# Routed feed-forward after attention on one core: the second layer's weights are split in the attention part and multiplied in three reduced-precision products

## What is computed

```python
x = x + xattn(layernorm(x), ctx)     # 16 heads of 32; keys = values = context; @ W_out.T + b
x = x + attn(layernorm(x), ...)      # 32x32 self attention, low-rank projections, rotary part, @ Wo + b
xf = layernorm(x)                    # the routed layer:
idx = argmax(softmax(xf @ Wg + bg))  # one expert of 8 for each row
h = gelu(xf @ W1[idx] + b1[idx], exact)
x = x + h @ W2[idx] + b2[idx]        # W1, W2: 8 x 512 x 512
```

## Time and profile before

| | |
|---|---|
| runs | 808.64 us median (805.21, 808.64, 811.38) |
| profiled execution | 810.45 us, its span (first to last instruction) 808.6 us |
| mean granted clock of PE | 0.970 of full speed |
| busy share of the span | PE 90%, PE weight loads 69%, DVE 72%, ACT 54%, POOL 42% |
| transfers | 129.06 MB, mean 160 GB/s; SP's queue 51.2% of the engines' time |
| chain that ended last | PE 62%, DVE 14%, DMA 8%, issue 6%, ACT 5% |

### The profile page before, as it was taken

How to read it: one execution, slowest core, us unless ns; L and a number is a source line. 1 busy time by engine, 2 the same in 40 slices (tenths; PEclk the granted TensorE clock), 3 DMA queues, 4 the chain that set the end, 5 groups by cost and what they waited for, 6 DMA issues and landing times.

```text
span 808.6 us, 26299 instructions
## 1 busy us (share of the span) xinstructions
PE 731.3 (90%) x10502; PEld 554.5 (69%) x10502; DVE 582.9 (72%) x1184; ACT 435.3 (54%) x1085; POOL 337.4 (42%) x687
## 2 busy tenths in 40 slices
PE   4978899998999989999999898999897879999997
PEld 3635677777877867777778687787686546666664
DVE  3458376878878788778787777877547547788983
ACT  2335265756667557565666565765423435555552
POOL 1202343435344434353444434443404357866652
PEclk9899699999999999999999999999998989999999
DMA  9954266567576765775756647561241997544420
GB/s 278 343 119 106 67 149 143 137 159 183 133 175 145 161 152 141 159 180 126 188 140 158 156 123 180 140 162 56 82 167 53 329 389 284 180 152 137 142 104 4
DMA packets 114376, 129.06 MB, mean 160 GB/s; under 512 B 14478, under 2 KB 81294, under 8 KB 114256
## 3 DMA queue, kind: packets, MB, share of 16 engines
q1 hardware_dynamic: 105984, 109.26, 51.2%
q0 software_dynamic: 5520, 16.26, 5.7%
q10 hardware_dynamic: 2752, 1.86, 0.9%
HBM read 114.77 MB, written 14.42 MB: 160 GB/s over the span
## 4 chain that ended last, share of the span: by engine, by line
PE 62%; DVE 14%; DMA 8%; issue 6%; ACT 5%; SPq 2%; POOL 2%; ACTq 1%; DVEq 0%; POOLq 0%
PE stage_banks L1642 9%; PE stage_banks L539 6%; DMA keys<-in_ctx 6%; PE stage_banks L541 5%; PE stage_banks L540 5%; PE scores L590 5%; PE att_bank L614 4%; PE stage_banks L533 3%; PE scores L600 3%; PE scores L1620 2%; PE scores L1622 2%; PE scores L1621 2%; SPq L457 2%; DVE k_t L1080 2%; PE stage_banks L546 2%
## 5 line engine op out<-in xcount | busy, mean ns | idle before, releaser
L875 ACT ACTIVATE prob<-scores,negmax 128x257 f32<-128x257 f32 x256 | 118.5, 476 | 45.5 <-DVE negmax L1090 45.5
L539 PE MATMUL stage_banks<-qkv_hi,operand_hi 128*128 128x398 f32 x256 | 98.1, 383 | 4.3 <-DVE operand_lo L1094 4.2
L1080 DVE STREAM_TRANSPOSE k_t<-keys 128x512 f32<-128x512 f32 x128 | 86.4, 686 | 16.9 <-DMA keys<-in_ctx 16.9
L540 PE MATMUL stage_banks<-qkv_lo,operand_hi 128*128 128x398 f32 x256 | 88.6, 346 | 0.0
L1090 DVE TENSOR_REDUCE negmax<-scores 128x2 f32<-128x514 f32 x128 | 82.9, 678 | 7.7 <-PE scores L590 7.4
L541 PE MATMUL stage_banks<-qkv_hi,operand_lo 128*128 128x398 f32 x256 | 88.4, 345 | 0.0
L600 PE MATMUL scores<-consts,prob 128*128 128x128 f32 x512 | 77.1, 278 | 12.1 <-ACT prob L875 12.1
L1642 PE MATMUL stage_banks<-w_all,hidden 128*128 x184 | 82.8, 592 | 0.6 <-ACT hidden L1695 0.6
L614 PEld LDWEIGHTS att_bank<-prob_t,context 128*32 128x32 f32 x4096 | 45.9, 114 | 50.0 <-issue 36.3
L600 PEld LDWEIGHTS scores<-consts,prob 128*128 128x128 f32 x512 | 60.1, 142 | 26.1 <-ACT prob L875 22.6
L1738 DVE TENSOR_TENSOR w_lo<-w_all,w_hi 128x512 fp32r<-128x512 f32 x89 | 76.8, 921 | 0.8 <-ACT w_hi L1674 0.3
(11 more groups left out here) (260 smaller groups left out, 1664.0 us busy)
## 6 DMA issues: line engine op xcount, KB each, us to landing
keys<-in_ctx SPq DMA_DIRECT2D x256, 128.0 KB, 4.6
context<-in_ctx SPq DMA_DIRECT2D x64, 512.0 KB, 4.6
w_all<-in_L_ffn_W SPq DMA_DIRECT2D x16, 1024.0 KB, 10.1
b<-in_L_ffn_b SPq DMA_DIRECT2D x23, 256.0 KB
norm_scratch<-norm SPq DMA_DIRECT2D x16, 256.0 KB
x_tile<-in_x SPq DMA_DIRECT2D x8, 256.0 KB, 3.0
x_pair<-in_x SPq DMA_DIRECT2D x8, 256.0 KB
x_scratch<-x_tile SPq DMA_DIRECT2D x8, 256.0 KB, 2.3
```

Source lines behind the costliest of these rows:

```text
L539: pe.matmul(to, op_hi[op][:, c, :], w_hi[name][:, c, columns], start=(c == 0), stop=False)
L540: pe.matmul(to, op_hi[op][:, c, :], w_lo[name][:, c, columns], start=False, stop=False)
L875: act.activation(prob[pair][:, gg, :], scores[:, g, 0:J], ACT.Exp, bias=negmax[b % 2][:, g:g + 1], accum_out=sums[t % 2][:, g, bl:bl + 1]) ...
L1080: dve.transpose(dst, src).then_inc(keys_turned, 1)
```

## The change

- **Second layer in three products.** `w_all` holds, for each expert, the high and the low part of W2 instead of W1 and W2. ACT cuts gelu's result into a high part (`hidden_hi`), DVE forms `hidden_lo`, each in two halves, and `second_layer` makes 12 F32R products in place of 4 plain ones.
- **W2 is split ahead of time.** In the attention part, at every 17th step from step 112 on, one of 32 pieces (128 rows of an expert's W2, 256 KB) is loaded by ACT's queue, copied to its high part and subtracted to its low part by POOL, and 512 KB stored to a DRAM scratch by ACT's queue. Expert 0 is loaded back at step `STEPS * (B + 1)`, experts 1 to 5 as buffers of the attention part come free, 6 and 7 in the expert part.
- **W1 is loaded for each slot**, 1 MB, into two buffers `first_raw`, two slots ahead.
- **The second bias** is fetched by index in the attention part (`TAKE_B2`, POOL) and added to x2 by POOL before x2 is stored (`ADD_B2`); `add_bias` and `load_bias` go. The stores of x2 and norm3 move from SP's queue to ACT's (`STORE2`, `STORE3`). x has five buffers (`NX = 5`), and `load_x` no longer waits for norm3.
- `move_first` goes from DVE to ACT, the order on ACT and DVE in a slot is another, there are more fill products (`RANK` 2 to 8, `SLOTS` 6 to 10), and buffers lie elsewhere.

```diff
-EARLY = 2
+LOAD_OF = (0, 1, 1, 2, 2, 2, 3, 4)
+NX = 5
+TAKE_B2, ADD_B2, STORE2, STORE3 = 109, 114, 117, 106
+SPLIT_FIRST, SPLIT_EVERY = 112, 17
+SPLIT_HI, SPLIT_LO, SPLIT_STORE = 10, 12, 15
-BEFORE = {..., "RANK": 2, "SLOTS": 6, "FIRST": 9}
+BEFORE = {..., "RANK": 8, "SLOTS": 10, "FIRST": 9}
 # SP
         def load_x(t):
-            if t >= 4:
-                until.wait_ge(x2_stored[t % 4], 16 * (t // 4))
-                until.wait_ge(normed_r, t - 3)
+            if t >= NX:
+                until.wait_ge(x2_stored[t % NX], 16 * (t // NX))
...
-                sp.dma_start(x2_dram[t * P:(t + 1) * P, :], x_tile[t % 4][:, :])...
-                sp.dma_start(norm3_dram[t * P:(t + 1) * P, :], norm3[:, :])...
             if step == STEPS * (B + 1):
...
-                for e in range(EARLY):
+                until.wait_ge(w2_stored, 16 * G)
+                load_expert(sp, 0)
+                sp.dma_start(first_raw[0][:, :, :], ins["L0_ffn_W1"][0]...).then_inc(first_loaded[0], 16)
+                until.wait_ge(xout_done, T)
+                until.wait_ge(att_used, T)
+                until.wait_ge(w2_stored, 16 * E * G)
+                for e in (1, 2):
+                    load_expert(sp, e)
+                until.wait_ge(qkv_done, 4 * T)
+                until.wait_ge(self_scored, T)
+                for e in (3, 4, 5):
                     load_expert(sp, e)
 # ACT, attention part
+            t = tile_at(step, STORE3, LATER["STORE3"])   # wait normed_r t+1, store norm3
+            t = tile_at(step, STORE2, LATER["STORE2"])   # wait x2_biased t+1, store x2
+            n = split_at(step, 0)
+                until.wait_ge(w2_made, 2 * n)
+                act.dma_start(w2_whole, ins["L0_ffn_W2"][e, m * P:(m + 1) * P, :]).then_inc(w2_loaded, 16)
+            n = split_at(step, SPLIT_STORE)
+                until.wait_ge(w2_made, 2 * n + 2)
+                act.dma_start(w2_dram[e, :, :, m, :], w2_part).then_inc(w2_stored, 16)
 # POOL, attention part
+            t = tile_at(step, TAKE_B2, LATER["TAKE_B2"])
+                until.wait_ge(expert_known, t + 1)
+                pool.indirect_dma_start(b2_rows[:, :], None, ins["L0_ffn_b2"][:, :], ...top_at...).then_inc(b2_taken, 16)
+            t = tile_at(step, ADD_B2, LATER["ADD_B2"])
+                until.wait_ge(b2_taken, 16 * (t + 1))
+                pool.tensor_tensor(x_tile[t % NX][:, :], x_tile[t % NX][:, :], b2_rows[:, :], ALU.add).then_inc(x2_biased, 1)
+            n = split_at(step, SPLIT_HI)
+                until.wait_ge(w2_loaded, 16 * (n + 1))
+                pool.tensor_copy(w2_part[:, 0, :].bitcast(F32R), w2_whole).then_inc(w2_made, 1)
+            n = split_at(step, SPLIT_LO)
+                pool.tensor_tensor(w2_part[:, 1, :].bitcast(F32R), w2_whole, w2_part[:, 0, :], ALU.subtract).then_inc(w2_made, 1)
 # SP, expert part
+        def load_first(s):
+            if s >= 2:
+                until.wait_ge(w1_low, G * (s - 1) - 2)
+                until.wait_ge(w1_low_first, 2)
+            at = sp.value_load(of_slot_i[0:1, s:s + 1], ...)
+            sp.dma_start(first_raw[s % 2]..., ins["L0_ffn_W1"][bass.ds(at, 1), :, :]...).then_inc(first_loaded[s % 2], 16)
+        load_first(1)
         for s in range(SLOTS):
+            if s == 0:   # wait for norm3 rows of 4 slots and x2 rows of 4 slots
+            if s in (0, 2):
+                load_expert(sp, 6 + s // 2)
             if s + 2 < SLOTS:
-                load_bias(s + 2)
+                load_first(s + 2)
 # PE, second_layer
             for m in range(G):
-                done = pe.matmul(bank[:, :], hidden[s % 2][:, m, :], w_of[..., 1, m, :]..., start=(m == 0), stop=(m == G - 1))
+                until.wait_ge(hidden_high, 2 * s + m // 2 + 1)
+                pe.matmul(bank[:, :], hi[:, m, :], high, start=(m == 0), stop=False)
+                pe.matmul(bank[:, :], hi[:, m, :], low, start=False, stop=False)
+                until.wait_ge(hidden_low, 2 * s + m // 2 + 1)
+                done = pe.matmul(bank[:, :], lo[:, m, :], high, start=False, stop=(m == G - 1))
 # ACT, expert part
         for s in range(SLOTS):
             if s + 1 < SLOTS:
-                split_rows(s + 1)
-                split_first(s + 1)
+                split_first(s + 1, range(3))
+            move_first(s)
+            if s + 1 < SLOTS:
+                split_first(s + 1, (3,))
+            for half in range(2):   # two gelus, wait for them, one cut of 128x256 into hidden_hi
+            if s + 2 < SLOTS:
+                split_rows(s + 2)
 # DVE, expert part
         for s in range(SLOTS):
             if s + 1 < SLOTS:
                 lower_first(s + 1, range(G))
             if s:
                 add_rows(s - 1)
             if s + 1 < SLOTS:
                 move_b1(s + 1)
+            lower_hidden(s)         # two subtractions of 128x256
+            if s + 2 < SLOTS:
+                lower_rows(s + 2)
 # POOL, expert part: add_bias gone; before the gathers it waits for all x2 rows, as before
```

More of the change, by code:

```diff
@@ L189, in part_at, with split_at, program @@
     return -1, 0
+def split_at(step, offset):
+    n, rest = divmod(step - offset - SPLIT_FIRST, SPLIT_EVERY)
+    return n if rest == 0 and 0 <= n < E * G else -1
 def units_at(step):
     return [n for n, at in enumerate(UNIT_AT) if at == step]
-def program(nc, ins, out, const_at, x2_dram, norm3_dram):
+def program(nc, ins, out, const_at, x2_dram, norm3_dram, w2_dram):
     ctx = ExitStack()
@@ L346, in program @@
     const_loaded, tables_loaded, last_loaded = signal("const_loaded"), signal("tables_loaded"), signal("last_loaded")
-    x_loaded = [signal(f"x_loaded{i}") for i in range(4)]
+    x_loaded = [signal(f"x_loaded{i}") for i in range(NX)]
     context_loaded = [signal(f"context_loaded{i}") for i in range(4)]
@@ L1505, in program @@
     first = [sb(f"first{i}", [P, FI]) for i in range(2)]
-    hidden = [sb(f"hidden{i}", [P, G, P]) for i in range(2)]
+    first_raw.append(sb("first_raw1", [P, G, FI]))
     routing = ExitStack()
@@ L1517, in program @@
     routing.close()
-    b2_loaded = [signal(f"b2_loaded{i}") for i in range(2)]
+    hidden_hi, hidden_lo = ([sb(f"{n}{i}", [P, G, P], F32R) for i in range(2)] for n in ("hidden_hi", "hidden_lo"))
+    hidden = [sb(f"hidden{i}", [P, G, P]) for i in range(2)]
     rows_gathered = [signal(f"rows_gathered{i}") for i in range(NR)]
@@ L1541, in attention_over, with rows_stored, loaded_to, first_layer_loaded @@
         until.wait_ge(rstd_r, T)
-    def loaded_to(until, s, layers):
+    def rows_stored(until):
+        for i in range(NX):
+            until.wait_ge(x2_stored[i], 16 * ((T - 1 - i) // NX + 1))
+    def loaded_to(until, s):
         for e in range(min(s, E - 1) + 1):
-            until.wait_ge(expert_loaded[e], 16 if e == EARLY else 32)
-        if layers == 2 and s >= EARLY:
-            until.wait_ge(second_loaded, 16)
+            until.wait_ge(expert_loaded[LOAD_OF[e]], 16 * LOAD_OF.count(LOAD_OF[e]))
+    def first_layer_loaded(until, s):
+        until.wait_ge(first_loaded[s % 2], 16 * (s // 2 + 1))
     def expert_sync_program():
@@ L1636, in second_layer @@
                 until.wait_ge(known, PUT_AT)
-            loaded_to(until, s, 2)
+            loaded_to(until, s)
             until.wait_ge(known, EXPERTS)
             place = pe.value_load(at_i[0:1, s:s + 1], min_val=0, max_val=E - 1)
+            hi, lo = hidden_hi[s % 2], hidden_lo[s % 2]
             for m in range(G):
-                until.wait_ge(gelu_done, G * s + m + 1)
-                done = pe.matmul(bank[:, :], hidden[s % 2][:, m, :], w_of[:, bass.ds(place, 1), 1, m, :].rearrange("p a n -> p (a n)"),
-                                 start=(m == 0), stop=(m == G - 1))
+                high, low = (w_of[:, bass.ds(place, 1), part, m, :].rearrange("p a n -> p (a n)").bitcast(F32R) for part in range(2))
+                until.wait_ge(hidden_high, 2 * s + m // 2 + 1)
[3 more added lines that the diff above has]
+                done = pe.matmul(bank[:, :], lo[:, m, :], high, start=False, stop=(m == G - 1))
             done.then_inc(second_done, 1)
```

231 lines of the change are left out of this document (121 added, 110 removed).

## The result

The changed kernel took **853.34 us** (median of four: 846.53, 848.43, 858.25, 862.44) against 810.01 for the kernel before on the same chip: ratio **1.052, 95% interval 1.0463 to 1.0576**. Forecast were 797 us and a range of 783 to 811. The execution of 862.44 us ran in a slower state (granted clock 0.938, where the two fastest have 0.953), and the ratio leaves it out. It is the one that was profiled (span 860.3): the other three are 4 to 16 us shorter, about 0.3 to 1.2 us a tile.

A forecast was written before the change was run, and what follows sets the result against it. PE was taken to bound the expert slots, with full DMA in the first slots and small waits in attention. From 810.45 us, -15.2 - 3 + 2 + 0.7 - 6 + 5 + 3 = -13.5 gave 797 us, range 783 to 811.

The forecast's parts named there:

- The failed step: Attention part, POOL: added subtractions, copies, gathers and additions, 114 us of work, cost +3 us, bounds 0 and +15.
- The sign of being wrong: Attention part: a tile of 33.5 us or more, with ACT or POOL in the chain, would show the forecast wrong.
- Second layer, -15.2: Expert part: 12 reduced products replace four plain ones, 0.66 us saved in each of 23 slots, -15.2 us.
- slot stays near 7: Rival, expert part: late W1 or ACT's round keeps slots at 6.7 to 7.0 us, total 804 to 811; chance 0.22.
- ACT's thin slack: Expert part: ACT's move ends at 11.1 us, next turn_first due at 11.9; slack 0.8 us, holding barely.
- three passes for four: Second layer: counting passes through the array, reduced products would save 19.8 us instead of the 15.2 taken.
- First slots, -3: Start of expert part: of 9.3 us lost, some 6 come back as W1 loads late; -3, bounds -9 and +3.
- End of attention and routing, +2, bounds 0 and 4: The last tile's bias chain (fetch, landing, addition, store) delays ACT's W1 cuts and the first gather: +2 us.
- SP unblocked, -6, bounds 0 and -9: Attention part: without SP's wait for norm3, keys come in time and PE's 7.7 us at L784 can go: -6.
- ACT's 96 issues, +5: Attention part: 64 W2 issues and 32 stores, 42 us on ACT, an eighth reaching PE: +5, bounds 0 and +35.
- The rival with a chance of 0.13: ACT's issues: at 1.0 us each, a third reaching PE, 96 cost 32 us, total 824; chance 0.13.
- POOL's added work, +3: Attention part: 114 us more on POOL, busy 13.8 of 33, with long gaps: +3, bounds 0 and +15.

The follow-up runs named there:

- neither: The changed kernel without the second bias's fetch and addition and without the split of W2 (loaded directly): 787.7 us, ratio 0.9732 to the kernel before.
- Run 11: The changed kernel with split, bias addition and x2 store later, plus SP loading W1 of slots 1 and 2 first, experts 6 and 7 in pieces: 802.4 us.
- kernel 1: The changed kernel without the indexed fetch and addition of the second bias, x2 stored without it: 809.7 us, ratio 1.0018 to the kernel before.
- run 12: Run 11's kernel with the last but one tile's x2 store later and experts 3 to 5 loaded one by one, 4 and 5 after bias fetches: 803.9 us.
- Run 13: The kernel before with x2 and norm3 stored from ACT's queue and five x buffers, nothing else of the change: 794.5 us, ratio 0.9823.
- run 7: "neither" plus the split's 64 transfers from ACT's queue, loads waiting for nothing, no split work on POOL: 792.3 us, ratio 0.9805 to the kernel before.
- run 6: "neither" plus the split's transfers from ACT's queue, each load waiting for the store two steps before it, nothing on POOL: 867.55 us, ratio 1.0732.

## Why the prediction was wrong

**The failed step** is, in its words, on POOL: "its order carries last-key copies, the reciprocal deviation and the wait for b2_taken: +3, bounds 0 and +15". I named the wait, named what stands behind it, and then priced the pair as if little more than POOL's busy time counted. POOL's second wait, that of `SPLIT_HI` for its piece, has no term at all. The sign of being wrong that I had named, a tile of 33.5 us or more with ACT or POOL in the chain, is what came: 36.7, and POOL is 17% of the chain of after. What the runs put in its place, from 787.7 ("neither") up to 853.3:

| fetch | split | us | tile, us | PE's wait for `norm_x`, us |
|---|---|---|---|---|
| none | none | 787.7 | 31.5 | none |
| none | POOL's work alone | 795.4 | 32.1 | 2.3 |
| none | transfers alone | 792.3 | 31.9 | none |
| as changed | none | 794.6 | 31.8 | 3.5 |
| none | as changed | 809.7 | 33.5 | 7.0 |
| late | late | 807.1 | 33.05 | 6.5 |
| late | as changed | 821.7 | 33.9 | 9.9 |
| as changed | late | 837.6 | 34.95 | 20.5 |
| as changed | as changed | 853.3 | 36.7 | 26.8 |

The last row's tile and wait are those of the execution of 862.44 us.

Time over 787.7 and PE's wait for `norm_x` grow together, 2.0 to 3.4 us of time for one of wait. Part of that factor is the lower clock behind a wait; PE's waits for key copies (7.5 us in after, none in "neither") and for `norm_w` (7.4 and 5.2) and the end of the attention part have their share, which I have not divided up. That is a correlation over nine kernels; the separate causes are the differences between rows.

**Why fetch and split cost 65.6 together and 6.9 and 22.0 alone.** The runs show that it is so and that the place of the addition and of the x2 store behind it decides most of it: moved, they win back 31.6 of the fetch's 43.6 us. The traces give a reason, which is an argument from them. ACT waits for `shift_x` in every tile of "neither" too (24.1 us, 14 times, longest 1.9), and PE never waits for it: there is slack. Without the split the fetch lands 4.1 us after its issue (median, 100 to 540 us) and POOL waits at most 2.5 us for it; ACT's wait grows to 35.8 us and PE's only to 3.5. With the split the landing takes 5.9 us, POOL's wait reaches 5.9, and a cast and a subtraction stand between it and the deviation: the slack is used up and what comes on top reaches PE. How much is due to the later landing and how much to the added operations is not separated; no run had the fetch beside the transfers alone. Nor is how much came by ACT's store of x2, which waits for the addition ahead of the norm: in the tile shown it was issued at 210.59 us, and the norm behind it began only at 215.33, after the deviation.

**The other terms.**
- *Second layer, -15.2*: right. 6.43 us a slot was forecast as 6.4 (23 x 0.62 = 14.3 measured), so no other engine is in the way: the rival "slot stays near 7" is out, ACT's thin slack held, and the DMA share of 0.83 is the forecast 82%. The products start 0.234 us apart (759.38 to 761.95 for 11 steps); the alternative of three passes for four, -19.8, was wrong, as the earlier trace rows said.
- *First slots, -3*: 38.5 us against 37.5, of which four slots at 6.43 against 7.05 explain -2.5. So the surplus over four slots rose from 9.3 to 12.8 us: +3.5, just outside my upper bound of +3. W1 of slot 2 was late, as said: ACT waited 8.5 us for it in after, and PE 4.9 us for the move that stands behind those cuts in ACT's order, where I had said about 5. What failed is that the rest of the stall did not go: PE also waited 2.7 us for ACT's move in slot 0, and its granted clock was 0.67 from 700 to 720 us. Run 11 confirms the part of W1.
- *End of attention and routing, +2, bounds 0 and 4*: wrong, and by the same error. The chain I had written down (fetch, landing, addition, store) was priced with a landing of "3 or so". Experts 1 and 2, and then 3 to 5, 10 MB, are on the queues there, and the trace of after has
```profile
645.14 1.27 POOL L1446 TENSOR_TENSOR x_pair<-x_pair,staged_c 128x512 f32<-128x512 f32 x1 [8.04 <-DMA staged_c<-in_L_ffn_b,top_at]
675.53 0.81 ACT L859 ACTIVATE norm<-x_tile,shift_r,rstd_r 128x512 f32<-128x512 f32 x1 [12.16 <-DMA norm_scratch<-norm]
```
  8.04 us for one bias and 12.16 for the store of norm3, 256 KB each. The second is also in kernel 1, without any bias (11.4 us). In after it has a twin: ACT's store of x2, next ahead in its order, was issued at 675.10 us, when POOL had made the addition that it waits for (673.81 + 1.26), so a prompt landing of norm3 alone would have gained next to nothing there. From the last ranking product to slot 0 pass 17.2 us in place of 13.1, and more lies ahead of that product. I don't put one number on it, since run 12 shows that the wait moves when it is chased.
- *SP unblocked, -6, bounds 0 and -9*: right in kind, too small, and outside my bound. Run 13 has 14.5 us for it alone (809.06 to 794.51; 10 to 18 by the interval). The waits of the earlier trace rows that I named are gone in it, which fits the mechanism; the fifth x buffer came with it. The Trainium skill, page "DMA: Bandwidth & Descriptors", section "Issuing engines are not separate DMA queues", would have had about zero for that move. The run decides for the row: what was saved is not issue time but an in-order wait of SP.
- *ACT's 96 issues, +5*: right, though the eighth in it was a guess. 64 of them with their 24 MB cost 4.6 us, the other 32 are inside run 13's gain. In after a load of W2 took ACT's queue 0.33 to 1.53 us to issue (median 0.49), a store of a split piece 0.52 to 0.59, at a DMA share of 0.73. The rival with a chance of 0.13, and its price of 1.0 us an issue, was wrong: single issues cost that, the usual one half.
- *POOL's added work, +3*: the split's busy time was 7.7, inside the bounds. The waits were not.

In sum: "neither" (profiled 788.75) is near the forecast's gains: the terms -15.2, -3 and -6 against 810.45 give 786. That is luck in part. In its trace the last ranking product starts at 603.3 us, 13.0 earlier than before, and slot 4 follows slot 0 after 39.2 us instead of 37.5: SP's term was too small by about what the first slots' term was too good. Of the 65.6 us above "neither", 12.3 are the split's work and bytes, for which the forecast had some 8; the other 53 come with the fetch and, by what is left over, with POOL's waits for pieces, and they are the miss. The rival that ended slower had the wrong engine: ACT's issues, where it was POOL's waits, and so the range had no case for them.

## What to carry to other kernels

A wait for a landing on an in-order compute engine is priced by what stands behind it, not by that engine's load: list the next few instructions, find the one that another engine needs soonest, and compare the landing *at the DMA share that the change itself makes* with that slack. Put such consumers behind the urgent work (here ten steps later, with the store that waits for them, 31.6 us), and look for the reverse as well: here one queue's wait taken off SP made the kernel before 14 us faster, where the whole change in its best complete form (run 11) is 6 us faster than it. When two additions share one slack, their prices alone say nothing about their price together.

## What the runs showed of the hardware

- Transfers of 256 KB land late behind large ones of other queues: the fetched bias took 4.1 us (median) at a DMA share of 0.66 without the split, 5.9 at 0.73 with it; beside the expert loads a wait for one was 8.04 us, and for a store of 256 KB 12.16 us in after and 11.4 in kernel 1.
- A DMA share of 0.80 with 24 MB more took PE only 3.5 us of 440 when no engine stood long for a landing (run 7), where a wait of ACT for each store made the kernel 80 us slower than "neither" (run 6).
- After waits of 1.70 and 3.62 us within 7 us the granted clock was 0.50 until about 221.5 us: PE's products started 0.33 us apart 12 times, and then 0.18 us apart. The slower stretch adds 1.8 us to the waits.
- DVE's subtractions of a cut took 2.65 us for four in after (740.29), with no POOL addition beside them, against 4.34 before with one.
